# Second layer's projections: value products beside the rotated queries, biases added on 512 columns

## The chip, the cores and the metric

The kernel runs on one core of a Trainium2 chip. The metric is device time in microseconds (us), from launch to end. Engines: PE (TensorE, matrix products; PEld is its loading of weights), DVE (VectorE), ACT (ScalarE), POOL (GpSimd) and SP (SyncE, which issues DMAs here).

## The reference, cut to what matters

Four layers run one after the other on `x` of 4 x 512 x 256. The change is in the first part of the second layer. For each of four batches of 512 normalised tokens `xn` (256 features) this part computes:

```python
kv_d = xn @ Wkv_d.T + bkv_d          # 64 latent features
q_d  = xn @ Wq_d.T  + bq_d           # 64 latent features
k1 = kv_d @ Wk_u.T + bk_u            # 128
q1 = q_d  @ Wq_u.T + bq_u            # 128
v  = kv_d @ Wv_u.T + bv_u            # 256
kr = rope(xn  @ Wrk.T + brk)         # 128
qr = rope(q_d @ Wrq.T + brq)         # 128
S  = softmax(xn @ router_w + router_b)   # gates of 16 experts
y0 = xn @ expert_w + expert_b            # one product for all experts, 256
```

After it come the attention of 16 heads on `k = (k1, kr)`, `q = (q1, qr)` and `v`, and the addition of `y0` weighted by the gates.

## The kernel before, in words

Everything is written out by hand: each engine has its own list of instructions, run in order, and engines wait for one another by semaphores. A layer is made of blocks; at a block's end all engines meet.

`project1` is the block in question. It goes through the batches b = 0 to 3. Tokens are transposed to `xnT` (features on rows, 512 columns); `latT` holds `kv_d` on rows 0 to 63 (`LO`) and `q_d` on rows 64 to 127 (`HI`), and `w.up` holds the weights that act on each on the same rows. A product with only 64 contracted rows uses half of the array's rows.

PE's list for one batch is:

- the latent product (L837), 16 columns of router logits for each of four token tiles (L839), and the two halves of the rotary keys (L844, L845), all of 128 contracted rows;
- from `latT`: `k1` (L849, rows LO) and `q1` (L850, rows HI), then the two halves of the rotary queries (L851, L852, both rows HI), into banks 2 to 5;
- for each of four token tiles t: the expert product, 256 columns into the left half of bank 2 + t (L857), and the values, 256 columns into its right half (L858, rows LO). The banks are those of `k1`, `q1` and the two halves of `qr`, so each t first waits until that bank was read. After t = 1 come the transposes of the gates (L866). In the last batch the first two units of attention scores (L829) follow t = 2 and t = 3;
- the transposes of the next batch's `xn` into banks 0 and 1 (L814).

All matrix products that go through the helper `product` carry its line, L803. Each f32 matmul is two MATMUL instructions in the profile.

ACT's list for one batch: copy of the first half of `xnT` (L713), `latT` (L715), the exponential of the gates (L717), `k1` and `q1` with biases (L720, L722), normalising the next batch's `xn` (L707, four instructions), rounding of keys and queries to bf16: `kq1`, `kqr` (L702), then after POOL's subtractions the second parts, `kq1`, the gates' copy (L734), `kqr` (L702). POOL's list: the output bias for `x` (L674), reciprocal roots (L668), two subtractions (L688) and two more (L692), 1024 columns each. SP then stores the parts.

DVE's list for one batch: copy of the second half of `xnT` (L763), statistics of the next batch, logits and their maximum (L768 to L771), rotation of the keys (L755, L758, L760), the gates (L780 to L782), rotation of the queries (the same three lines), and for each tile t the biases of `y0` and `values` (L789, L790), 256 columns each. Eight maxima over score units (L794, two banks each) close the list of the block.

`attend1` is the block after it.

Of the kernel before, what the change touches and what calls it, by code (L numbers as in the profile page):

```python
# [9 lines left out]
ALU = mybir.AluOpType  # L10
# [3 lines left out]
P = 128  # L14
B, S, C = 4, 512, 256
# [34 lines left out]
class Core:  # L50
# [8 lines left out]
    def sem(self, name):  # L59
        return self.ctx.enter_context(self.nc.semaphore(name))  # L60
# [527 lines left out]
def project1(k, y0, gateT, values, split, early):  # L588
# [4 lines left out]
    PAIRS = TT * LANES // 2  # L593
    B_LAT, B_K, B_KR, B_KRS, B_Q, B_QR, B_QRS = (w.columns[:, i:i + 1] for i in range(7))
    V_ROW, O_ROW, E_ROW = range(3)
    with ExitStack() as ctx:
        sb, sem = scoped(k, ctx, "l1a")
        stats = sb("stats", [P, TT, 6])
# [33 lines left out]
        q1_ready = sem("q1_ready")  # L632
        qrot_done = sem("qrot_done")
        y_read = sem("y_read")
        lmax_ready = sem("lmax_ready")
        gexp_ready = sem("gexp_ready")
        gate_ready = sem("gate_ready")
# [100 lines left out]
        @block.vector  # L738
        def _(dve):
            own = Own(dve, dve_own)  # L740
            dve.wait_ge(*k.groups["w1"])

            def statistics(b):
                norm_stats(k, dve, own, lambda t: k.x[:, b, t, :], stats, mv, rstd, var_ready)

            def shifts(b):
                dve.wait_ge(rstd_ready, b)
                nc.vector.scalar_tensor_tensor(shift[:, :], mv[:, :, 0], -1.0, rstd[:, :], ALU.mult, ALU.mult).then_inc(shift_ready, 1)

            for b in range(B):  # L750

                def rotate(side, made, done, cos_bank, sin_bank, bias, swapped_bias):

                    dve.wait_ge(made, b * 2 + 1)
                    nc.vector.scalar_tensor_tensor(kqr[:, side, :], ps[cos_bank][:, :], bias, w.rope[:, 0, :], ALU.add,  # L755
                                                   ALU.mult).then_inc(done, 1)
                    dve.wait_ge(made, b * 2 + 2)
                    own.link(nc.vector.scalar_tensor_tensor(turn[:, side, :], ps[sin_bank][:, :], swapped_bias,  # L758
                                                            w.rope[:, 1, :], ALU.add, ALU.mult))
                    nc.vector.tensor_tensor(kqr[:, side, :], kqr[:, side, :], turn[:, side, :], ALU.add).then_inc(done, 1)  # L760

                dve.wait_ge(xt_made, b * 2 + 2)
                nc.vector.tensor_copy(xnT[:, 1, :], ps[1][:, :]).then_inc(xt_dve, 1)  # L763
                if b + 1 < B:
                    statistics(b + 1)

                dve.wait_ge(logits_made, b + 1)
                own.link(nc.vector.tensor_tensor(logit[:, :, :], ps[1][:, 0:TT * EXPERTS].rearrange("p (t e) -> p t e", t=TT),  # L768
                                                 w.router_b[:, :].unsqueeze(1).broadcast_to([P, TT, EXPERTS]), ALU.add))
                own.link(nc.vector.tensor_reduce(lmax[:, :], logit[:, :, :], axis=AX.X, op=ALU.max))  # L770
                nc.vector.tensor_tensor(logit[:, :, :], logit[:, :, :],  # L771
                                        lmax[:, :].unsqueeze(2).broadcast_to([P, TT, EXPERTS]),
                                        ALU.subtract).then_inc(lmax_ready, 1)
                if b + 1 < B:
                    shifts(b + 1)
                dve.wait_ge(biased, b + 1)
                rotate(0, kr_made, krot_done, 7, 0, B_KR, B_KRS)

                dve.wait_ge(gexp_ready, b + 1)
                own.link(nc.vector.tensor_reduce(lsum[:, :], logit[:, :, :], axis=AX.X, op=ALU.add))  # L780
                own.link(nc.vector.reciprocal(lsum[:, :], lsum[:, :]))
                nc.vector.tensor_tensor(logit[:, :, :], logit[:, :, :],  # L782
                                        lsum[:, :].unsqueeze(2).broadcast_to([P, TT, EXPERTS]),
                                        ALU.mult).then_inc(gate_ready, 1)
                rotate(1, qr_made, qrot_done, 4, 5, B_QR, B_QRS)

                for t in range(TT):
                    dve.wait_ge(y_made, b * TT + (t + 1))
                    nc.vector.tensor_tensor(y0[:, b, t, :], ps[2 + t][:, 0:C], w.rows[:, E_ROW, :], ALU.add)  # L789
                    nc.vector.tensor_tensor(values[:, b, t, :], ps[2 + t][:, C:2 * C], w.rows[:, V_ROW, :],  # L790
                                            ALU.add).then_inc(y_read, 1)
            for i in range(PAIRS):
                dve.wait_ge(early.smax_made, i + 1)
                nc.vector.tensor_reduce(early.nmax[:, 0, 2 * i:2 * i + 2], k.pair(early.bank(i)), axis=AX.X, op=ALU.max,  # L794
                                        negate=True).then_inc(early.smax_read, 1)

        @block.tensor
        def _(pe):
            pe.wait_ge(*k.groups["w1"])

            def product(bank, weights, rhs):
                for c in range(CT):
                    last = nc.tensor.matmul(bank, weights(c), rhs(c), start=(c == 0), stop=(c == CT - 1))  # L803
                return last

            LO, HI = slice(0, L1_LAT), slice(L1_LAT, P)
            def turn_input(b):
                if b:
                    pe.wait_ge(xn_ready, b)
                    pe.wait_ge(krot_done, b * 2 - 1)  # L810
                    pe.wait_ge(lmax_ready, b)
                for c in range(CT):
                    for t in range(TT):
                        last = nc.tensor.transpose(ps[c][:, t * P:(t + 1) * P], xn[:, t, c * P:(c + 1) * P], k.ident[:, :])  # L814
                    last.then_inc(xt_made, 1)

            def first_scores(i):
                if i == 0:
                    pe.wait_ge(early.loaded[0], LOADS)
                    pe.wait_ge(krot_done, B * 2 - 1)  # L820
                    pe.wait_ge(lmax_ready, B)
                elif i == 1:
                    pe.wait_ge(gt_ready, B)
                    pe.wait_ge(lat_ready, B)
                else:
                    pe.wait_ge(early.smax_read, i - 1)
                for m in range(2):
                    t, j = divmod(2 * i + m, LANES)
                    last = nc.tensor.matmul(ps[early.bank(i) + m][:, :], early.KQ[0:ROWS, QUERY, 0, j, t * P:(t + 1) * P],  # L829
                                            early.KQ[0:ROWS, KEY, 0, j, :], start=True, stop=True)  # L830
                last.then_inc(early.smax_made, 1)

            turn_input(0)
            for b in range(B):
# [10 lines left out]
                product(ps[0][:, :], lambda c: w.rope_k[:, c, P:2 * P], lambda c: xnT[:, c, :]).then_inc(kr_made, 1)  # L845
                pe.wait_ge(lat_ready, b + 1)
                if b:
                    pe.wait_ge(y_read, b * TT)
                nc.tensor.matmul(ps[2][:, :], w.up[LO, 0:P], latT[LO, :], start=True, stop=True).then_inc(k1_made, 1)  # L849
                nc.tensor.matmul(ps[3][:, :], w.up[HI, 0:P], latT[HI, :], start=True, stop=True).then_inc(q1_made, 1)  # L850
                nc.tensor.matmul(ps[4][:, :], w.up[HI, P:2 * P], latT[HI, :], start=True, stop=True).then_inc(qr_made, 1)  # L851
                nc.tensor.matmul(ps[5][:, :], w.up[HI, 2 * P:3 * P], latT[HI, :], start=True, stop=True).then_inc(qr_made, 1)  # L852

                for t, (ready, value) in enumerate(((k1_ready, b + 1), (q1_ready, b + 1), (qrot_done, b * 2 + 1),
                                                    (qrot_done, b * 2 + 2))):
                    pe.wait_ge(ready, value)
                    product(ps[2 + t][:, 0:C], lambda c: xnT[:, c, t * P:(t + 1) * P], lambda c: w.expert[:, c, :])  # L857
                    nc.tensor.matmul(ps[2 + t][:, C:2 * C], latT[LO, t * P:(t + 1) * P], w.up[LO, P:3 * P],  # L858
                                     start=True, stop=True).then_inc(y_made, 1)
                    if b + 1 == B and t >= 2:  # L860
                        first_scores(t - 2)
                    if t == 1:
                        pe.wait_ge(gate_ready, b + 1)
                        pe.wait_ge(krot_done, b * 2 + 1)
                        for u in range(TT):
                            last = nc.tensor.transpose(ps[7][0:EXPERTS, u * P:(u + 1) * P], logit[:, u, :], k.ident[:, :])  # L866
                        last.then_inc(gt_made, 1)
                if b + 1 < B:
                    turn_input(b + 1)
            for i in range(2, PAIRS):  # L870
                first_scores(i)
            pe.wait_ge(y_read, B * TT)
            pe.wait_ge(early.smax_read, PAIRS)


# [1715 lines left out]
```

## Time and profile before

| | before |
|---|---|
| median of 3 runs | 1127.55 us (1126.84 to 1127.59) |
| the profiled execution's own time | 1129.45 us |
| its span, first to last instruction | 1127.7 us |
| PE busy | 958.3 us, 85% |
| DVE busy | 793.3 us, 70% |
| POOL busy | 474.9 us, 42% |
| ACT busy | 462.9 us, 41% |
| mean granted PE clock | 0.936 |

The span is what the profile shows in detail; the 1.75 us between it and the execution's own time lie around it. Busy shares are averages over four layers with different limits, so what a change in one stage is worth has to be read from that stage. The granted clock is 1.00 at 2.4 GHz and 0.50 at 1.2 GHz.

### The profile page before, as it was taken

How to read it: one execution, taken by the hardware profiler on the slowest of the kernel's cores; microseconds unless marked ns; L12 is line 12 of the kernel's file. 1: busy time of each engine (PE TensorE's matmuls, PEld its weight loads, DVE VectorE, ACT ScalarE, POOL GpSimd, SP SyncE). 2: the span in 40 equal slices, each digit the busy share in tenths (PEclk: the TensorE clock that was granted, in tenths of full speed). 3: DMA queues.
4: the chain of work that ended last, by engine and by line, in shares of the span. 5: the costliest groups of instructions: out<-in, count | busy, mean ns of one | idle time of the engine just before them, and what ended most of it. 6: DMA issues, size and time to landing. Idle time of an engine off the chain costs nothing. (4 is left out here: it accounts for less than half of the span.)

```text
span 1127.7 us, 12859 instructions
## 1 busy us (share of the span) xinstructions
PE 958.3 (85%) x4126; PEld 497.0 (44%) x4130; DVE 793.3 (70%) x1395; ACT 462.9 (41%) x764; POOL 474.9 (42%) x479
## 2 busy tenths in 40 slices
PE   5899699799999998579999958887888788879877
PEld 2566455323333332336556544235533553355424
DVE  3665665688787875276877647993799378947795
ACT  3233145256666666264654426112621252124411
POOL 2322167464444440143633511961196108810781
PEclk9999899889999999599999969998999899999899
DMA  8500024312212200300000010000000000000000
GB/s 296 192 15 15 15 92 143 107 34 59 74 48 69 53 15 1 133 1 15 1 15 15 1 40 0 1 1 20 0 0 0 20 0 0 0 20 0 0 0 19
DMA packets 28653, 43.11 MB, mean 38 GB/s; under 512 B 6480, under 2 KB 21792, under 8 KB 28192
## 3 DMA queue, kind: packets, MB, share of 16 engines
q1 hardware_dynamic: 28592, 42.41, 12.0%
q8 instruction: 25, 0.41, 0.2%
q14 instruction: 36, 0.29, 0.1%
HBM read 30.93 MB, written 11.27 MB: 37 GB/s over the span
## 5 line engine op out<-in xcount | busy, mean ns | idle before, releaser
L1095 DVE TENSOR_REDUCE l_nmax<-banks 128x1 f32<-128x512 f32 (+1 forms) x165 | 147.9, 930 | 35.1 <-PE banks L1198 33.9
L1054 ACT ACTIVATE l1b_PT<-banks 128x512 f32<-128x512 f32 (+1 forms) x176 | 134.3, 794 | 66.7 <-PE banks L1211 66.2
L2431 PE MATMUL banks<-l_scaled,l_cbm 128*128 128x512 f32 x224 | 123.7, 667 | 41.5 <-POOL l_scaled L2141 23.7
L2141 POOL TENSOR_TENSOR l_scaled<-l_X,l_source 128x512 f32<-128x512 f32 x112 | 134.6, 1227 | 0.0
L2310 DVE TENSOR_TENSOR banks<-banks,l_decay 128x512 f32<-128x512 f32 x128 | 88.1, 691 | 12.2 <-PE banks L2431 7.7
L2431 PEld LDWEIGHTS banks<-l_scaled,l_cbm 128*128 128x128 f32 x224 | 40.0, 204 | 113.2 <-POOL l_scaled L2141 82.2
L1198 PE MATMUL banks<-l_KQ 96*128 96x512 bf16 x240 | 81.8, 394 | 8.0 <-DVE l_nmax L1095 5.2
L2284 DVE TENSOR_TENSOR l_y<-l_y,banks 128x512 f32<-128x512 f32 x128 | 86.7, 677 | 1.9
L1211 PE MATMUL banks<-l_KQ 99*128 99x512 bf16 x256 | 85.5, 388 | 2.9 <-ACT l1b_PT L1054 2.1
L2210 ACT ACTIVATE l_hhi<-l_h 128x512 f16<-128x512 f32 (+1 forms) x24 | 15.2, 632 | 137.7 <-DVE l_h L2323 137.7
L1225 PE MATMUL banks<-l1b_PT,l1b_V 128*32 128x512 f32 x512 | 68.2, 605 | 0.0
L2128 POOL TENSOR_TENSOR l_across<-l_X,l_source 128x512 f32<-128x512 f32 x16 | 17.0, 1075 | 120.9 <-ACT l_X L2196 120.9
L2240 DVE SCALAR_TENSOR_TENSOR l_conv<-l_padded,w_taps,l_conv 128x512 f32<-128x512 f32 x72 | 52.7, 750 | 15.2 <-ACT l_conv L2186 13.5
L1770 PE MATMUL banks<-l_xhi,l_ternary 128*128 128x512 f16 x128 | 49.5, 387 | 6.3 <-DVE l_h L1700 6.3
L1211 PEld LDWEIGHTS banks<-l_KQ 99*128 99x128 bf16 x256 | 22.3, 100 | 64.5 <-ACT l1b_PT L1054 47.8
L1563 POOL TENSOR_TENSOR l_sqsum<-l_sqsum,l_sq 128x512 f32<-128x512 f32 x28 | 40.3, 1440 | 23.3 <-ACT l_sq L1603 22.2
L1770 PE MATMUL banks<-l_xlo,l_ternary 128*128 128x512 f16 x128 | 49.4, 386 | 0.0
L2374 PE MATMUL banks<-l_xnT,w_inner 128*128 128x512 f32 x96 | 48.8, 671 | 0.0
L1757 PE MATMUL banks<-l_xnT,w_qkv 128*128 128x512 f32 x96 | 44.5, 622 | 1.0 <-DVE l_xnT L1644 1.0
L390 PE MATMUL banks<-w_qkv,l_xnT 128*128 128x512 f32 x64 | 37.0, 733 | 8.9 <-DVE l_xnT L289 8.9
L1021 POOL TENSOR_SCALAR l1b_above<-l1b_gate,l1b_trial 128x256 f32<-128x256 f32 x45 | 41.0, 924 | 1.4 <-DMA l1b_gate<-l_gate 1.4
L1198 PEld LDWEIGHTS banks<-l_KQ 96*128 96x128 bf16 x240 | 22.7, 99 | 40.1 <-DVE l_nmax L1095 14.9
(325 smaller groups left out, 2056.1 us busy)
## 6 DMA issues: line engine op xcount, KB each, us to landing
l_split<-l1a_parts SPq DMA_DIRECT2D x16, 384.0 KB, 3.3
l_KQ<-l_split SPq DMA_DIRECT2D x48, 128.0 KB, 2.9
l_KQ<-l_split SPq DMA_DIRECT2D x16, 192.0 KB, 3.1
l_KQ<-l_split SPq DMA_DIRECT2D x48, 64.0 KB, 2.8
w_ternary<-l_tern_out SPq DMA_DIRECT2D x7, 384.0 KB, 2.3
x<-in_x SPq DMA_DIRECT2D x4, 512.0 KB, 9.4
l_raw<-in_w_gate_up SPq DMA_DIRECT2D x2, 1024.0 KB, 10.3
out<-x SPq DMA_DIRECT2D x4, 512.0 KB, 3.0
```

Source lines behind the costliest of these rows:

```text
L1054: nc.scalar.activation(PT[:, first:first + size, :], source, ACT.Exp, scale=SCALE).then_inc(p_ready, 1)
L1095: nc.vector.tensor_reduce(nmax[:, H % 2, first:first + size], source, axis=AX.X, op=ALU.max, negate=True).then_inc(smax_read, 1)
L1198: last = nc.tensor.matmul(ps[bank + m][:, :], KQ[pairs, QUERY, g, j, t * P:(t + 1) * P], KQ[pairs, KEY, g, j, :], start=True, stop=True)
L1211: last = nc.tensor.matmul(ps[KEY_BANK + bank + m][:, :], KQ[whole, KEY, g, j, kt * P:(kt + 1) * P], KQ[whole, QUERY, g, j, :], start=True, ...
L1225: last = nc.tensor.matmul(ps[OUT_BANK][j * LANE:(j + 1) * LANE, :], V[:, kt, g * LANES + j, :], PT[:, kt * LANES + j, :], start=(kt == 0), ...
L1770: last = nc.tensor.matmul(ps[2 * (j % 2) + part][:, :], gate_up[:, c, first:first + P], x[:, c, :], start=(c == 0 and x is xhi), stop=(c = ...
L2141: nc.gpsimd.tensor_tensor(by_head(scaled[:, n % 4, :]), by_head(X[:, T, :]), spread(source[:, level, T, :]), ALU.mult).then_inc(scaled_rea ...
L2240: last = nc.vector.scalar_tensor_tensor(conv[:, n, :], padded[:, n % 2, tap:tap + S], w.taps[:, n, tap:tap + 1], conv[:, n, :], ALU.mult, ...
L2284: nc.vector.tensor_tensor(y[:, T, :], y[:, T, :], ps[4 + n % 4][:, :], ALU.add).then_inc(prod_added, 1)
L2310: nc.vector.tensor_tensor(by_head(ps[4 + n % 4][:, :]), by_head(ps[4 + n % 4][:, :]), spread(decay[:, level, T, :]), ALU.mult).then_inc(pr ...
L2374: last = nc.tensor.matmul(ps[2 + n][:, :], w.inner[:, c, X0 + n * P:X0 + (n + 1) * P], xnT[:, c, :], start=(c == 0), stop=(c == CT - 1))
L2431: last = nc.tensor.matmul(bank, cbm[:, T % 2, level, :], scaled[:, own_n % 4, :], start=True, stop=True)
```

## The change

In `project1` alone:

- The four value products of a batch leave the loop over t. Two of them (256 columns each, rows LO) are issued behind each of the two products of the rotary queries (512 columns, rows HI). They write both halves of bank 6, then of bank 1.
- The expert products of t = 0 and 1 share bank 2, those of t = 2 and 3 share bank 3. They wait for the reading of `k1` and `q1`.
- DVE adds the biases on 512 columns: two instructions for the values, then two for `y0`, where there were eight of 256 columns.
- New waits of PE: before the rotary queries, for the query rotation of the batch before and for the logits' last step (`lmax_ready`); before the transposes, for the values' addition (`v_read`); before the first score units, the same. The counts of `y_read` go from 4 to 2 a batch.

```diff
-                for t in range(TT):
-                    dve.wait_ge(y_made, b * TT + (t + 1))
-                    nc.vector.tensor_tensor(y0[:, b, t, :], ps[2 + t][:, 0:C], w.rows[:, E_ROW, :], ALU.add)
-                    nc.vector.tensor_tensor(values[:, b, t, :], ps[2 + t][:, C:2 * C], w.rows[:, V_ROW, :],
-                                            ALU.add).then_inc(y_read, 1)
+                for half in range(2):
+                    dve.wait_ge(v_made, b * 2 + (half + 1))
+                    nc.vector.tensor_tensor(values[:, b, 2 * half:2 * half + 2, :], halves(ps[V_BANKS[half]][:, :]),
+                                            w.rows[:, V_ROW, :].unsqueeze(1).broadcast_to([P, 2, C]), ALU.add).then_inc(v_read, 1)
+                for half in range(2):
+                    dve.wait_ge(y_made, b * 2 + (half + 1))
+                    nc.vector.tensor_tensor(y0[:, b, 2 * half:2 * half + 2, :], halves(ps[2 + half][:, :]),
+                                            w.rows[:, E_ROW, :].unsqueeze(1).broadcast_to([P, 2, C]), ALU.add).then_inc(y_read, 1)
...
+                    pe.wait_ge(v_read, b * 2)
...
+                    pe.wait_ge(v_read, B * 2)
                 elif i == 1:
                     pe.wait_ge(gt_ready, B)
                     pe.wait_ge(lat_ready, B)
+                    pe.wait_ge(v_read, B * 2 - 1)
...
                 if b:
-                    pe.wait_ge(y_read, b * TT)
+                    pe.wait_ge(y_read, b * 2)
                 nc.tensor.matmul(ps[2][:, :], w.up[LO, 0:P], latT[LO, :], start=True, stop=True).then_inc(k1_made, 1)
                 nc.tensor.matmul(ps[3][:, :], w.up[HI, 0:P], latT[HI, :], start=True, stop=True).then_inc(q1_made, 1)
-                nc.tensor.matmul(ps[4][:, :], w.up[HI, P:2 * P], latT[HI, :], start=True, stop=True).then_inc(qr_made, 1)
-                nc.tensor.matmul(ps[5][:, :], w.up[HI, 2 * P:3 * P], latT[HI, :], start=True, stop=True).then_inc(qr_made, 1)
-
-                for t, (ready, value) in enumerate(((k1_ready, b + 1), (q1_ready, b + 1), (qrot_done, b * 2 + 1),
-                                                    (qrot_done, b * 2 + 2))):
+                if b:
+                    pe.wait_ge(qrot_done, b * 2)
+                pe.wait_ge(lmax_ready, b + 1)
+                for turned in range(2):
+                    nc.tensor.matmul(ps[4 + turned][:, :], w.up[HI, (1 + turned) * P:(2 + turned) * P], latT[HI, :],
+                                     start=True, stop=True).then_inc(qr_made, 1)
+                    for t in (2 * turned, 2 * turned + 1):
+                        last = nc.tensor.matmul(ps[V_BANKS[turned]][:, t % 2 * C:(t % 2 + 1) * C], latT[LO, t * P:(t + 1) * P],
+                                                w.up[LO, P:3 * P], start=True, stop=True)
+                    last.then_inc(v_made, 1)
+
+                for t, (ready, value) in enumerate(((k1_ready, b + 1), (k1_ready, b + 1), (q1_ready, b + 1), (q1_ready, b + 1))):
                     pe.wait_ge(ready, value)
-                    product(ps[2 + t][:, 0:C], lambda c: xnT[:, c, t * P:(t + 1) * P], lambda c: w.expert[:, c, :])
-                    nc.tensor.matmul(ps[2 + t][:, C:2 * C], latT[LO, t * P:(t + 1) * P], w.up[LO, P:3 * P],
-                                     start=True, stop=True).then_inc(y_made, 1)
+                    last = product(ps[2 + t // 2][:, t % 2 * C:(t % 2 + 1) * C], lambda c: xnT[:, c, t * P:(t + 1) * P],
+                                   lambda c: w.expert[:, c, :])
+                    if t % 2:
+                        last.then_inc(y_made, 1)
```

## Rows read from the trace of the kernel before

**Rows 1.** Busy time by stretch: the block; columns PE, PEld, DVE, ACT, POOL, clock, DMA.
```profile
136.60:224.10 87.50, 78.09 (x304) 41.29 (x304) 53.80 (x122) 35.00 (x52) 54.95 (x36) 0.97 0.35 109
```

**Rows 2.** Timeline of PE, second batch: start us, us, then bracketed idle time.
```profile
157.64 1.96 PE L803 MATMUL banks<-l1a_xnT,w_latent 128*128 128x512 f32 x4 [0.87 <-DVE l1a_xnT L763]
159.44 1.85 PE L803 MATMUL banks<-w_router,l1a_xnT 128*128 128x16 f32 x16
161.14 3.68 PE L803 MATMUL banks<-l1a_xnT,w_rope_k 128*128 128x512 f32 x8
164.75 0.69 PE L849 MATMUL banks<-l1a_latT,w_up 64*128 64x512 f32 x1
164.76 0.69 PE L850 MATMUL banks<-l1a_latT,w_up 64*128 64x512 f32 x1
165.28 0.59 PE L849 MATMUL banks<-l1a_latT,w_up 64*128 64x512 f32 x1
...
165.72 1.02 PE L851 MATMUL banks<-l1a_latT,w_up 64*128 64x512 f32 x2
...
167.53 1.13 PE L803 MATMUL banks<-w_expert,l1a_xnT 128*128 128x256 f32 x4
168.59 0.70 PE L858 MATMUL banks<-w_up,l1a_latT 64*128 64x256 f32 x2
...
170.90 0.60 PE L866 MATMUL banks<-ident,l1a_logit 128*16 128x128 f32 x4
171.34 1.03 PE L803 MATMUL banks<-w_expert,l1a_xnT 128*128 128x256 f32 x4
...
174.61 1.09 PE L814 MATMUL banks<-ident,x 128*128 128x128 f32 x8
176.58 0.67 PE L803 MATMUL banks<-l1a_xnT,w_latent 128*128 128x512 f32 x1 [0.88 <-DVE l1a_xnT L763]
```

**Rows 3.** Timeline of ACT and POOL, from the second batch's `k1` to the next copy.
```profile
165.97 0.69 ACT L720 ACTIVATE l1a_kq<-banks,w_columns 128x512 f32<-128x512 f32 x1 [3.10 <-PE banks L849]
...
169.10 1.05 ACT L702 ACTIVATE l1a_parts<-l1a_kq 128x1024 bf16<-128x1024 f32 x1
...
170.23 2.13 POOL L688 TENSOR_TENSOR l1a_kq<-l1a_kq,l1a_parts 128x1024 f32<-128x1024 f32 x1 [6.75 <-ACT l1a_parts L702]
...
174.48 1.06 ACT L702 ACTIVATE l1a_parts<-l1a_kqr 128x1024 bf16<-128x1024 f32 x1 [0.55 <-POOL l1a_kqr L688]
...
175.44 0.58 ACT L713 ACTIVATE l1a_xnT<-banks 128x512 f32<-128x512 f32 x1
```

**Rows 4.** Timeline of DVE, second batch.
```profile
168.42 0.69 DVE L760 TENSOR_TENSOR l1a_kqr<-l1a_kqr,l1a_turn 128x512 f32<-128x512 f32 x1
...
175.74 0.69 DVE L763 COPY l1a_xnT<-banks 128x512 f32<-128x512 f32 x1 [0.27 <-PE banks L814]
```

**Rows 5.** Timeline of the block's end, last batch.
```profile
205.40 1.13 PE L803 MATMUL banks<-w_expert,l1a_xnT 128*128 128x256 f32 x4
...
209.97 0.57 ACT L734 ACTIVATE l_gateT<-banks 16x512 f32<-16x512 f32 x1
...
213.61 9.32 DVE L794 TENSOR_REDUCE l_nmax<-banks 128x2 f32<-128x1024 f32 x8
```

**Rows 6.** Waits of SP in the block: total, times, longest.
```profile
SPq L596 <- PEq L596: 4.1, 1, 4.1
```

**Rows 7.** Busy time by stretch around idle PE; columns as in rows 1.
```profile
37.10:39.86 2.76, 0.00 (x1) 0.03 (x1) 2.69 (x7) 0.00 (x0) 1.07 (x1) 1.00 0.96 261
40.62:44.04 3.42, 3.42 (x5) 1.35 (x4) 3.30 (x10) 0.66 (x2) 0.00 (x0) 0.50 0.39 158
503.31:505.45 2.14, 0.00 (x0) 0.00 (x0) 2.04 (x6) 0.81 (x2) 1.68 (x2) 1.00 0.00 0
777.90:788.14 10.24, 6.98 (x21) 4.95 (x22) 3.44 (x5) 1.47 (x2) 2.12 (x1) 0.50 0.01 2
781.16:784.80 3.64, 3.64 (x17) 3.64 (x18) 0.00 (x0) 1.00 (x1) 2.12 (x1) 0.50 0.00 0
1096.82:1099.27 2.45, 0.00 (x2) 0.01 (x1) 2.45 (x5) 1.25 (x3) 0.58 (x1) 1.00 0.00 0
```

More of the change, by code:

```diff
@@ L595, in project1 @@
     V_ROW, O_ROW, E_ROW = range(3)
+    V_BANKS = (6, 1)
     with ExitStack() as ctx:
@@ L634, in project1 @@
         y_read = sem("y_read")
+        v_made = sem("v_made")
+        v_read = sem("v_read")
         lmax_ready = sem("lmax_ready")
@@ L871, in _ @@
                 first_scores(i)
-            pe.wait_ge(y_read, B * TT)
+            pe.wait_ge(y_read, B * 2)
             pe.wait_ge(early.smax_read, PAIRS)
```

## The prediction

> **What bounds the kernel now.** I read the shares first and put them aside: they are averages over four layers. The table by stretch gives the block of the change 87.5 us, with PE busy 78.09 of them at a mean clock of 0.97 [rows 1]; the other layers are not touched and follow in sequence, so their times only shift. Then I read PE's timeline for one batch. From one latent product to the next are 176.58 - 157.64 = 18.94 us, and PE idles only once in them, 0.88 us, between the transposes and the next latent product, where DVE's copy L763 is the last of what it waits for [rows 2]. So PE paces the block. The question is what comes second, and how close behind.
>
> The timeline of ACT and POOL answers it [rows 3]. ACT waits for `k1` until 165.97. From there it has no slack: both additions and the normalising, then rounding at 169.10, which releases POOL at 170.23; POOL needs two subtractions of 2.13 us; ACT rounds the second part from 174.48, for which it waited 0.55 us on POOL; and only then, at 175.44, comes its copy of the next `xnT` in its list, done at 175.44 + 0.58 = 176.02. DVE's copy ends at 175.74 + 0.69 = 176.43 [rows 4]. The second path is 0.41 us behind the first. It starts at `k1` and does not contain one product that the change moves.
>
> **The change on PE.** A tile's step is now expert 168.59 - 167.53 = 1.06 us, then values up to the next expert. From the first expert to the transposes are 174.61 - 167.53 = 7.08 us, in which the gates' transposes take 171.34 - 170.90 = 0.44 [rows 2]. Each tile therefore takes (7.08 - 0.44)/4 = 1.66 us, of which the values hold 0.60. What an expert product costs without a change between whole and half array behind it, the rows show only through the latent product, four instructions of 512 columns in 159.44 - 157.64 = 1.80 us, so about 0.88 for 256 columns [rows 2]. After the change: 4 x 0.88 + 0.44 = about 4.0 us for 7.1, 3.1 us less on PE in a batch, if the values cost nothing in their new place.
>
> Do they? `k1` and `q1` are such a pair: rows LO and HI, first instructions at 164.75 and 164.76, both products done in 165.72 - 164.75 = 0.97 us, where the two rotary query products, both on rows HI, take 167.53 - 165.72 = 1.81 us [rows 2]. Two value products of 256 columns are as long as one rotary query product of 512. Lower bound nothing, as in the pair; upper bound their own time alone, 4 x 0.44 = 1.8 us a batch. I take nothing, the pair being the same kind of work on the same tile shapes.
>
> The Trainium skill speaks against that on its page "TensorE: Matmul & The Clock Gate" (section "The mechanism"): matmuls start and end strictly in program order. The trace disagrees for the two instructions of one product: the second of L849 starts at 165.28, behind the first of L850 at 164.76 [rows 2]. By the page's rule a value pair could begin only with the second half of its query product, which would cost some 0.6 us more a batch; this changes little below.
>
> The new waits of PE cost nothing. The query rotation of the batch before and `lmax_ready` are done long before. `v_read` stands before the transposes: DVE ends the query rotation at 168.42 + 0.69 = 169.11, then two additions of 0.69 us (the price of L760, 512 columns; upper bound 0.75, lower 0.58, L713's on ACT) give 170.5 [rows 3, 4]; the transposes would come at 167.53 + 4.0 = 171.5. The `y0` additions end near 172.3, within the 1.0 us of the transposes, so that DVE's copy isn't late. DVE's time goes from eight additions of 256 columns to four of 512, and is off the path either way.
>
> **What the loop gives.** The transposes end at 172.5 in place of 175.6, and DVE's copy at 173.2. ACT's copy remains at 176.02, because its whole chain hangs on `k1`. The next latent product starts some 0.12 us after that, at 176.14 in place of 176.58: the gain is about 0.4 us a batch, in three passages 1.2 us, not 3 x 3.1. (Lower bound 0, if ACT and POOL run a little slower beside a busier DVE; upper 3.1 each, if the chain weren't there.) The other 2.7 us become idle time of PE: 0.88 + 3.1 - 0.44 = 3.6 us at each passage.
>
> **The last batch** has no passage behind it. Counted in the time of before: experts from 205.40, two tiles to 207.2, gates' transposes to 207.6, the third tile to 208.5, score unit 0 (0.45 us) to 209.0, the fourth to 209.9. DVE's second `y0` addition goes from 210.0 to 210.7, and the first maximum starts there instead of at 213.61; score unit 1 waits for ACT's copy of the gates, which ends at 209.97 + 0.57 = 210.54, and is done at 211.1, in time for the second maximum [rows 5]. The eight maxima, 9.32 us, follow without a gap, so the block's end gains 213.61 - 210.7 = 2.9 us. SP's last store does not take it back: SP waited 4.1 us at the block's end [rows 6].
>
> Without anything else the sum is -1.2 - 2.9 = -4.1 us.
>
> **What idle time does to PE's clock.** Here I choose against the sum. Before the block, PE idled 2.76 us at 37.10 at a clock of 1.00; from 40.62, after it had resumed, the granted clock was 0.50 for 3.42 us with PE busy all the while [rows 7]. That is 1.2 in place of 2.4 GHz. Outside stretches where the clock was low already, the trace has fifteen idle stretches of PE of 2.39 us or more behind its first product, from that at 37.10 to that at 1096.82; all but the last were followed by such a drop, that one (2.45 us) kept 1.00 [rows 7]. Idle stretches near 2 us mostly keep it, as that at 503.31 does (2.14 us). The block has had none between batches. The change makes three, of 3.6 us each.
>
> The drop would cost half of what it covers of PE's work before `k1`, which is on the path: latent 1.8, router 1.7, rotary keys 3.6, `k1` 1.0, together 8.1 us [rows 2]. How long it lasts depends on what PE does. With dense products of 512 columns behind the gap it was 3.42 us, a cost of 1.7. With small products (16 instructions of 64 columns from 781.16 to 784.80) the low clock went on through them and 3.34 us into the dense products, to 788.14, 7.0 us after PE had resumed [rows 7]. Here 1.8 us of dense latent products come first, 3.6 at half clock, then the router's 16 instructions of 16 columns, 3.4 at half clock, then dense ones. If the clock returns during the latent products, a passage costs 1.7 us; if it stays for the router and 3.34 us more, 3.6 + 3.4 + 3.34 = 10.3 us low, it costs 5.1. I take the middle, 3.4, for some of each: 3 x 3.4 = +10.2 us. What PE does after `k1` may run slower too: it has 3.6 us to spare there.
>
> Forecast: -4.1 + 10.2 = +6.1 us. The profiled execution took 1129.45 us (span 1127.7 and 1.75 around it), so its like would be 1135.5; on the median 1127.55, which is 1.9 lower, 1133.6 us. With 1.7 at each passage it is +1.0 (1128.6), with 5.1 it is +11.2 (1138.8).
>
> **The rivals.** *The clock holds.* Then -4.1 us, 1123.5. For it: the idle stretch at 1096.82, and that the block's products are dense on both sides. Against: the fourteen others, and that 3.6 us is longer than half of them. Chance 0.10. *One drop in three, or all of them brief and late.* -4.1 + one passage of 1.7 to 5.1: within 2 us of now, 1125 to 1128.6. Chance 0.12. *The values are not hidden* but take 1.8 us a batch behind the queries. PE then idles 3.6 - 1.8 = 1.8 us at a passage, like the stretch that kept its clock; the loop still gains 1.2, the last batch 2.9 - 1.8 = 1.1: -2.3 us, 1125.3. Against it is the pair `k1`, `q1`. Chance 0.05. *ACT's chain is shorter than I read* (its order lets the copy through): each batch gains up to 3.1 us, -9.3 - 2.9 = -12.2, 1115.4. Against it: ACT's list is fixed in order, and the copy began at the very end of the rounding. Chance 0.03. The rest, 0.70, is the forecast: the sign turns where a passage costs more than 4.1/3 = 1.4 us, that is, where PE works 2.8 us at half clock before `k1` in each.
>
> **How the numbers follow.** What a measurement of this kernel can tell from no change is about 0.2%, 2.25 us. Of the forecast's 0.70, 0.61 lies above +2.25 and 0.09 within. Faster: 0.10 + 0.03 + half of 0.05, 0.15. Same: 0.12 + 0.09 + the other half, 0.23. Slower: 0.62. The likeliest case's own range is 1128.6 to 1138.8. The range of all reaches down to the case of hidden gains without a drop in part (1125.0) and up to the upper end with 2 us for a low stretch that falls worse into the start of the attention: 1141.0.
>
> **What would show it.** In the changed kernel's timeline: L849 and L851 at the same distance from the latent product wherever the clock is 1.00; value products beside L851's successors with the experts no later than 1.9 us after these begin; PE idle 3 to 3.7 us before each of three latent products, released by ACT's L713 and no longer by DVE's L763; 10.1 to 10.2 us from ACT's L720 to the end of L713, as now; and a granted clock of 0.50 over the latent products of batches 1 to 3. I am wrong if the clock stays at 1.00 there, if the idle time is under 2.4 us, or if L713 comes before ACT's last rounding.

## The result: faster, with the forecast on the wrong side

| | before | changed |
|---|---|---|
| median of 8 runs each, same chip | 1128.34 us (1126.84 to 1133.87) | 1123.37 us (1121.03 to 1127.02) |
| ratio | | 0.9956 (0.9936 to 0.9976) |
| the profiled execution's own time, span | 1129.45, 1127.7 us | 1127.02, 1125.2 us |
| mean granted PE clock | 0.936 | 0.932 |

The forecast was 1133.6 us, 6.1 slower; measured are 5.0 us less. The time is outside the range, 1125.0 to 1141.0 us, which left out two of the prediction's own rivals (1123.5 and 1115.4 us).

The first profile of the changed kernel happens to be the slowest of its eight executions. Its timeline of PE, second batch into the third (start us, us, idle time before in brackets; L809 is the helper that was L803):

```profile
156.76 3.23 PE L809 MATMUL banks<-l1a_xnT,w_latent 128*128 128x512 f32 x4 [3.58 <-ACT l1a_xnT L716]
...
161.96 3.68 PE L809 MATMUL banks<-l1a_xnT,w_rope_k 128*128 128x512 f32 x8
165.57 0.69 PE L858 MATMUL banks<-l1a_latT,w_up 64*128 64x512 f32 x1
...
166.53 0.38 PE L867 MATMUL banks<-w_up,l1a_latT 64*128 64x256 f32 x1
166.54 0.59 PE L864 MATMUL banks<-l1a_latT,w_up 64*128 64x512 f32 x1
...
168.35 1.99 PE L809 MATMUL banks<-w_expert,l1a_xnT 128*128 128x256 f32 x8
...
172.34 1.04 PE L821 MATMUL banks<-ident,x 128*128 128x128 f32 x8
176.88 2.87 PE L809 MATMUL banks<-l1a_xnT,w_latent 128*128 128x512 f32 x4 [3.50 <-ACT l1a_xnT L716]
```

Against [rows 2]: value products (L867) and rotary queries (L864) start together, though the values are listed behind both instructions of the query product, and queries and values take 168.35 - 166.53 = 1.82 us, as the queries alone did. PE now idles 3.5 us ahead of the latent product, and what ends the idle time is ACT's copy. ACT's timeline has the chain unchanged, 176.25 + 0.58 - 166.79 = 10.04 us against 10.05 in [rows 3]:

```profile
166.79 0.69 ACT L723 ACTIVATE l1a_kq<-banks,w_columns 128x512 f32<-128x512 f32 x1 [3.62 <-PE banks L858]
...
175.29 1.06 ACT L705 ACTIVATE l1a_parts<-l1a_kqr 128x1024 bf16<-128x1024 f32 x1 [0.55 <-POOL l1a_kqr L691]
176.25 0.58 ACT L716 ACTIVATE l1a_xnT<-banks 128x512 f32<-128x512 f32 x1
```

DVE's copy, last in [rows 4], is now done early. In the last batch the maxima start 218.82 - 210.80 = 8.02 us after `k1`, where it was 10.99 [rows 5, with `k1` at 202.62], and SP still waits for PE at the block's end, 1.2 us against 4.1 in [rows 6]:

```profile
173.42 0.69 DVE L766 COPY l1a_xnT<-banks 128x512 f32<-128x512 f32 x1 [0.18 <-PE banks L821]
...
218.82 9.32 DVE L800 TENSOR_REDUCE l_nmax<-banks 128x2 f32<-128x1024 f32 x8
```
```profile
SPq L597 <- PEq L597: 1.2, 1, 1.2
```

By stretches (span, busy time of PE, PEld, DVE, ACT, POOL, then clock and DMA) the block and its idle and low-clock stretches, to be read beside [rows 1, 7]:

```profile
133.41:229.81 96.40, 79.19 (x305) 48.26 (x305) 52.60 (x108) 34.92 (x52) 55.22 (x38) 0.82 0.35 99
153.20:156.76 3.56, 0.00 (x1) 0.00 (x1) 3.41 (x10) 2.95 (x4) 3.56 (x2) 1.00 0.00 0
157.36:160.78 3.42, 3.42 (x10) 1.86 (x8) 0.00 (x0) 0.69 (x1) 3.42 (x4) 0.50 0.80 262
177.84:188.08 10.24, 10.24 (x26) 6.10 (x24) 1.49 (x5) 0.94 (x2) 5.28 (x6) 0.50 0.55 172
201.72:208.56 6.84, 6.84 (x22) 4.76 (x21) 0.67 (x3) 0.94 (x2) 3.89 (x5) 0.50 0.68 230
```

So the mechanism forecast for the block is there: 3.5 us idle, and the clock at 1.2 GHz behind each. The block is not shorter but 8.6 us longer here. The gain must lie elsewhere. Cutting each profile at the first transposes of every part (the block ends at the next block's first product, which waits for POOL's `l1b_ident`) shows where. "Latent to `k1`" is the distance of the latent product from `k1` in the four batches; the lines below the first two are the experiments that follow:

| profile | block | latent to `k1` | third layer | fourth layer |
|---|---|---|---|---|
| before, first | 87.8 | 7.1, 7.1, 7.1, 7.1 | 194.5 | 463.9 |
| changed, first | 96.4 | 9.1, 8.8, 12.2, 10.5 | 191.6 | 460.3 |
| before, again | 87.9 | 7.1, 7.1, 7.1, 7.1 | 196.8 | 470.5 |
| changed, again | 88.4 | 7.1, 8.6, 8.8, 8.8 | 191.7 | 460.5 |
| changed, third | 88.4 | 7.1, 8.7, 8.8, 8.8 | 191.8 | 460.6 |
| changed, 16 memsets, first | 96.3 | 9.1, 8.8, 12.2, 10.5 | 192.8 | 465.2 |
| changed, 16 memsets, again | 88.3 | 7.1, 8.6, 8.8, 8.8 | 193.0 | 465.6 |
| before, wide additions | 88.9 | 7.1, 7.1, 7.1, 7.1 | 191.4 | 460.3 |

The fourth layer, whose code is the same, is 3.6 to 10 us shorter. It is the only part written as a loop over the batches. DVE's first copy in it, over the run before, four times (idle time ahead of it in us, and how often):

```profile
L2234 DVE COPY l_xnT<-banks x4: 691/692/692, 665.9 to 1012.2; 128x512 f32<-128x512 f32 x4
its engine sat idle before it (us, times) until:
  issue: 14.8, 3
```

In the changed kernel's third profile the same copy (the "issue" sums are of the copies into this tile alone):

```profile
L2251 DVE COPY l_xnT<-banks x4: 692/692/693, 660.6 to 1004.9; 128x512 f32<-128x512 f32 x4
its engine sat idle before it (us, times) until:
  issue: 8.4, 3
```

At each of the three turns of the loop DVE stood 4.9 us before and stands 2.8 us now, and it waited for nothing that the profile shows ("issue"). PE waits for that copy.

### The profile page after: what moved, and what is told of

Read it like the earlier page. It is cut to its first block and busy times, and to the rows that moved or that the text cites. A ratio compares the mean times of both kernels' runs of the same rounds, so it can differ in the third digit from the quotient of the medians.

```text
span 1125.2 us, 12850 instructions
## 1 busy us (share of the span) xinstructions
PE 951.4 (85%) x4126; PEld 499.1 (44%) x4130; DVE 793.8 (71%) x1379; ACT 461.5 (41%) x764; POOL 474.4 (42%) x479
## 5 line engine op out<-in xcount | busy, mean ns | idle before, releaser
L390 PE MATMUL banks<-w_qkv,l_xnT 128*128 128x512 f32 x64 | 32.0, 648 | 8.8 <-DVE l_xnT L289 8.8
```

## The experiments

### What in the change makes it faster

**Sixteen memsets back (e1_pad, and e10_pad beside e9_after).** DVE's list is 16 instructions shorter in the changed kernel. This puts 16 back, four per batch (0.08 us each four):

```diff
                                         ALU.subtract).then_inc(lmax_ready, 1)
+                for i in range(4):
+                    nc.vector.memset(spare[:, i:i + 1], 0.0)
```

> The changed kernel with sixteen more instructions in DVE's list of the block (four memsets of one spare column per batch, behind the logits' last step, where DVE has about 1 us to spare), so that DVE's list in front of the fourth layer's loop is as long as before the change (967 instructions, against 951 in the changed kernel). Theory A (the change was faster because the loop of the fourth layer now stands elsewhere in DVE's list: its first copy waits 2.6 to 2.8 us at each of three turns, put down to issue, where before it waited 4.8 to 5.1): the long waits come back, 3 x 2.2 = 6.7 us, so about 1130 us, slower than the kernel before by about 2. Theory B (the time was won in the block itself, the fourth layer's waits are chance): nothing changes, 1123.4 us, 5 less than before.

Measured: 1128.98 us, ratio to before 0.9982 (0.9960 to 1.0003). The gain is gone; that it would be 2 us slower than before did not show. Since the changed kernel had been timed on another chip, both were timed again on one:

> The changed kernel, unchanged, timed beside the next one on the same chip: 0.994 to 0.996 of the kernel before, 1123 us. Its block in a third profile: 88 to 97 us, with the latent product's start preceded by 3.5 us of idle PE and a clock of 0.50 over it in two or three of three passages.

> The changed kernel with the sixteen memsets again, so that DVE's list of the fourth layer stands where it stood before the change; on the same chip as the changed kernel itself. Theory A (the gain lies in the fourth layer's turns): 4 to 7 us slower than the changed kernel, and within 0.3% of the kernel before, since the block costs between +0.5 us (passages at 8.7 us, as in the changed kernel's second profile) and +8.6 us (as in its first). Theory B: no slower than the changed kernel.

Measured: changed 1121.83 us, 0.9938 (0.9911 to 0.9965); with the memsets 1129.08 us, 0.9990 (0.9967 to 1.0014). Sixteen memsets cost 7.3 us, and the waits at the turns are back:

```profile
L2254 DVE COPY l_xnT<-banks x4: 692/692/692, 663.6 to 1011.8; 128x512 f32<-128x512 f32 x4
its engine sat idle before it (us, times) until:
  issue: 14.9, 3
```

The change itself, with the list where it was, makes no difference that can be measured.

**The wide additions alone (e2_wide).** PE's list as before; DVE adds over pairs of banks:

```diff
-                for t in range(TT):
-                    dve.wait_ge(y_made, b * TT + (t + 1))
...
+                for half in range(2):
+                    dve.wait_ge(y_made, b * TT + 2 * half + 2)
+                    made = k.pair(2 + 2 * half)
+                    nc.vector.tensor_tensor(y0[:, b, 2 * half:2 * half + 2, :], made[:, :, 0:C],
+                                            w.rows[:, E_ROW, :].unsqueeze(1).broadcast_to([P, 2, C]), ALU.add)
```

> The kernel before with only the second part of the change: biases added on 512 columns (left halves of banks 2 and 3 as one instruction, right halves as one, then banks 4 and 5), PE's list as before. DVE's list is 16 instructions shorter. Theory A: the fourth layer's turns lose 3 x 2.2 = 6.7 us, the block loses up to 0.3 us at each passage because the last two additions (0.69 us each) end behind the transposes; together about 6, 1122.5 us, with PE's own part of the change absent. Theory B (the gain is in PE's reordered products): 1128 to 1129 us, as before.

Measured: 1122.38 us, 0.9926 (0.9899 to 0.9954). The reordered products are not needed for the gain. The block is 1.1 us longer than before (88.9 against 87.8), a little more than expected: 0.5 us by three periods of 19.11 us against 18.94, the rest at its ends.

### What the idle time costs, and what bounds the block

**The idle time filled (e3_fill).** Behind the transposes of each next batch:

```diff
+                if b:
+                    for _ in range(3):
+                        nc.tensor.matmul(ps[5][:, :], w.up[:, 0:P], w.rope[:, 0, :], start=True, stop=True)
```

> The changed kernel with three idle-time products (f32, 512 columns, constant operands, into bank 5, whose result nobody reads) behind the transposes of batches 1 to 3: 2.6 us of PE work in the 3.5 us in which PE would idle. Theory C (the idle time lowers PE's clock and this costs 3.4 us a passage, 1.7 to 5.0 in the profile of the changed kernel): the clock stays at 1.00 over the latent products, the distance from latent product to k1 is 7.1 us again, and the time falls by 5 to 10 us, to about 1115. If the drop costs little in most executions, the time stays at 1123.

Measured: 1114.54 us, 0.9858 (0.9828 to 0.9887), 9 us less than the changed kernel by the medians, which were taken on two chips; the changed kernel's one execution on this chip took 1122.46 us, 8 us more. PE's timeline of this kernel, second passage:

```profile
168.98 1.04 PE L821 MATMUL banks<-ident,x 128*128 128x128 f32 x8
169.85 2.74 PE L825 MATMUL banks<-w_rope,w_up 128*128 128x512 f32 x6
173.53 0.70 PE L809 MATMUL banks<-l1a_xnT,w_latent 128*128 128x512 f32 x1 [0.94 <-ACT l1a_xnT L716]
```

and its block in the table by stretches:

```profile
134.53:218.00 83.47, 73.24 (x323) 43.94 (x324) 53.13 (x108) 34.93 (x52) 55.32 (x38) 0.97 0.39 114
```

The clock holds between the batches, periods are 18.46 to 18.52 us, latent to `k1` 7.1 in all four. The block is 4.4 us shorter than before; the sum without the clock was -4.1. Useless products make the kernel faster. Against the changed kernel's second and third profile the block is 4.9 us shorter, against its first 12.9 us; the rest of the 9 us lies outside the block and its cause isn't shown.

**ACT's copy ahead (e4_order), and the shifts behind the rotation (e5_shift).**

```diff
+                if b + 1 < B:
+                    copy_turned(b + 1)
                 act.wait_ge(rest_ready, b * 2 + 1)
                 round_part(b, 0, kq1, 1, second_ready)
```

> The changed kernel with ACT's copy of the next xnT moved ahead of its two last roundings, into the time in which ACT waits for POOL. Theory D (the path behind PE is ACT's list from k1 over POOL's two subtractions to that copy, 10.1 us): DVE's copy is again last, PE idles under 2.4 us, the clock holds, and the batch takes 16 to 17 us instead of 18.5 plus the clock's cost; then POOL and DVE's rotations bound it. 3 x (2 + 3.4) = 16 us less, about 1107. Rival: POOL's list alone needs the time, the passage stays near 18.5 and the time within 3 us of 1123.

Measured: 1114.73 us, 0.9848 (0.9812 to 0.9885), less of a gain than expected. The profiled execution (1117.86 us) is one of the slower of the six, 1109.63 to 1118.70. Its second passage shows why, in the timeline of DVE, and below it in that of PE:

```profile
164.11 0.16 DVE L756 SCALAR_TENSOR_TENSOR l1a_shift<-l1a_mv,l1a_rstd 128x4 f32<-128x4 f32 x1 [3.65 <-POOL l1a_rstd L671]
```
```profile
171.73 1.60 PE L826 MATMUL banks<-ident,x 128*128 128x128 f32 x8 [2.41 <-DVE l_values L797]
```

With a shorter period DVE waits for POOL's reciprocal root ahead of the rotation, the values are added late, and `v_read`, the wait that the change added, holds the transposes. PE idles 2.41 us, the clock falls, and that batch has 12.8 us from latent to `k1`. So:

```diff
-                if b + 1 < B:
-                    shifts(b + 1)
                 dve.wait_ge(biased, b + 1)
                 rotate(0, kr_made, krot_done, 7, 0, B_KR, B_KRS)
+                if b + 1 < B:
+                    shifts(b + 1)
```

> As the kernel with ACT's copy moved ahead (1114.7 us), and DVE computes the next batch's shifts behind the rotation of the keys instead of ahead of it. In that kernel's profile the second passage still had PE idle 2.41 us, because DVE waited 3.6 us for POOL's reciprocal root ahead of the rotation and so added the values late; the clock fell for 13.7 us and the passage took 21.5 us. Theory: without that wait in front of the rotation the transposes are not late, PE idles under 1 us at each passage (released by DVE's copy), the clock stays at 1.00 behind the first batch, and the three passages take 16 to 16.5 us each, against 18.93 before the change: block 87.8 - 3 x 2.7 - 2.9 = about 77, time about 1107 us. Rival: another list (POOL's four operations and the bias, 12.3 us a batch, or ACT's second roundings) bounds it near 17.8 to 18.5 us a passage, and the time is 1110 to 1113.

Measured: 1107.01 us, 0.9812 (0.9786 to 0.9838). The passages take 15.79 us each, the block 75.5; PE is the bound again:

```profile
164.67 1.04 PE L826 MATMUL banks<-ident,x 128*128 128x128 f32 x8
166.58 1.96 PE L814 MATMUL banks<-l1a_xnT,w_latent 128*128 128x512 f32 x4 [0.88 <-DVE l1a_xnT L771]
```
```profile
133.00:208.50 75.50, 66.30 (x305) 40.91 (x306) 55.13 (x108) 34.58 (x52) 55.30 (x38) 0.95 0.41 126
```

This is what the change is worth once the second path is moved out of its way: 18.94 - 15.79 = 3.15 us a passage, and I had estimated 3.1 us less on PE. The kernel before with these two moves alone was not run; PE idled only 0.88 us a batch in it.

**Both kernels once more, for second profiles (e7_before, e8_after).**

> The kernel before once more, unchanged, for a second profile. Where the clock falls in the first, third and fourth layer differs from execution to execution; the block has no drop before its last scores (87.8 us again within 0.3), and the waits at the fourth layer's turns are 4.8 to 5.1 us again. If the change's gain in the fourth layer were chance, these waits would differ here.

> The changed kernel once more, unchanged, for a second profile. The first one was the slowest of its eight executions. If the cost of the clock in the block differs between executions, the distances from latent product to k1 differ from 8.8, 12.2 and 10.5 us here and the block is shorter than 96.4 us (92 if a passage costs 1.7 to 3); if it is always the same, they repeat.

Measured in single runs: 1134.61 and 1122.46 us. The waits at the turns are 5.1, 4.9 and 4.9 us before, 2.6 to 2.8 in the changed kernel. The clock's cost in the block does differ: here it falls for 3.4 us a passage, 1.5, 1.7 and 1.7 us of latent to `k1`, and the block is 88.4 us. The timeline and the stretch of the third passage:

```profile
176.56 3.65 PE L809 MATMUL banks<-l1a_xnT,w_latent 128*128 128x512 f32 x4 [3.50 <-ACT l1a_xnT L716]
```
```profile
176.74:180.14 3.40, 3.40 (x6) 1.33 (x6) 0.30 (x1) 0.00 (x0) 3.40 (x4) 0.50 1.02 286
```

### Why sixteen instructions count

By the written lists, DVE's first copy of the fourth layer is its instruction 967 before and 951 in the changed kernel, counted from 0; the loop has some 283. The DMA queues at the first turn of the kernel before (packets, MB, share of 16 engines), from 1.5 us ahead of the transposes to 5 us behind their start:

```profile
q1 hardware_dynamic: 528, 0.52, 23.9%
q14 instruction: 2, 0.02, 0.7%
```

The store of `x` goes out at just this turn (528 packets on its queue), with instruction packets on both sides of it. These start at 775.89 and 778.61 us, the store's packets start between 776.37 and 778.0, and DVE starts at 780.32. In the changed kernel's third profile the first two instruction packets start at 776.22 and 777.56, both ahead of the store's first at 777.75, and DVE starts at 779.50. The second packets, each in a window of half a microsecond, 778.23 to 778.73 before and 777.12 to 777.62 in the changed kernel:

```profile
q14 instruction: 1, 0.01, 3.8%
```
```profile
q14 instruction: 1, 0.01, 3.9%
```

In all their profiles, at every turn, DVE's copy starts 1.7 to 2.1 us behind the second packet. So 4.9 us against 2.8 goes with whether the store stands between the two packets; no run without the store tests it. More memsets move the loop on:

> The kernel before with sixteen more instructions in DVE's list (the same memsets): the fourth layer's first copy of DVE stands at 983 instead of 967. If what counts is the position within a stretch of 32 instructions, it is as good as the changed kernel's 951: the waits at the three turns are 2.6 to 2.9 us and the time about 6 less than before. If a longer list is simply a later one, or a longer stretch counts, the waits stay at 4.8 to 5.1 us and the time at 1128 to 1130.

> The kernel before with 64 more instructions in DVE's list; the fourth layer's first copy stands at 1031. Known are 951 (waits of 2.6 to 2.9 us), 967 (4.8 to 5.1) and 983 (1.6). If the position within a stretch of 64 counts, the waits are those of 967 again, 4.8 to 5.1 us. If it is within 32, the same; if only a longer stretch counts, they are others.

> The kernel with ACT's copy ahead and the shifts behind the rotation (1107.0 us), with 32 memsets of a spare column added to DVE's list, so that the fourth layer's first copy stands at 983, where the padded kernel before had it (waits at the turns of 1.6 us, put down to PE, in place of 2.6 to 2.9; fourth layer 455.4 us in place of 460). Theory: 4 to 5 us less, 1102 to 1103 us, 0.977 of the kernel before. If the position acted only together with the old PE list: 1107 again.

At 983 the kernel before takes 1121.04 us, 0.9933 (0.9901 to 0.9964), and DVE waits 1.64, 1.63 and 1.63 us, for PE's transposes:

```profile
775.68 0.69 DVE L2237 COPY l_xnT<-banks 128x512 f32<-128x512 f32 x1 [1.64 <-PE banks L2366]
```

No instruction packets run at its turns. At 1031 it is the same, 1.63 us (1121.27 us in one run), so the period is neither 32 nor 64, with which 1031 would be as slow as 967. On top of the best kernel, position 983 brought nothing: 1108.56 us, 0.9810 (0.9781 to 0.9838), though its waits fell to 1.6. Its fourth layer took 463.1 us in the profile against 460.4, with PE's clock low for about 76 us in it against 56, summed over the stretches. That expectation was a miss: a shorter turn also moves where the clock falls.

What was left: a longer period, 128 or 256, the length alone, or something short. With memsets at the head of DVE's list, in the first layer:

> The kernel before with 256 memsets of spare columns at the head of DVE's list in the first layer, where DVE waits for its data; the fourth layer's first copy stands at 1223 = 967 + 256. Theory F (DVE's list is fetched in blocks of 256, two of them stay, and the loop of 283 instructions is refetched at each turn when it touches three; the Trainium skill's page "Runtime: NRT & Kernel Launch", section "Instruction fetch mechanics", says so): the long waits come back, 4.8 to 5.1 us at three turns, with instruction packets on the DMA queue beside the store of x, and the time is 1128 to 1134 us. Rival (the waits belong to the old length alone): 1.6 us as at 983 and 1031, time 1118 to 1122.

> The same with 160 memsets; the fourth layer's first copy stands at 1127. Theory F: 967 and 951 touch three blocks, 983 to about 1200 touch two, so here the waits at the turns are 1.6 us, no instruction packets run there, and the time is 1118 to 1122 us. Rival (a period of less than 256 that 951, 967, 983 and 1031 happen to fit): some longer wait, 2.6 to 5.1 us.

Measured at 1223: 1133.78 us, 1.0044 (1.0030 to 1.0058), waits of 5.15, 5.07 and 4.96 us, instruction packets back at each turn. The medians are 4.8 us apart. The block starts at 139.74 us here and at 132.98 to 138.37 in the other profiles, so a part of them is what 256 memsets cost in the first layer. The queues at its first turn:

```profile
q1 hardware_dynamic: 528, 0.52, 24.0%
q14 instruction: 2, 0.02, 1.1%
```

At 1127: 1122.13 us, 0.9909 (0.9875 to 0.9943), waits of 1.68, 1.63 and 1.62 us, and the queues of its first turn are

```profile
q1 hardware_dynamic: 528, 0.52, 23.8%
```

951, 967 and 1223 are slow, 983, 1031 and 1127 fast. That fits a fetch in blocks of 256 of which DVE keeps two: a loop of 283 touches either two or three. The Trainium skill, on its page "Runtime: NRT & Kernel Launch" (section "Instruction fetch mechanics"), gives these two figures and says that a taken branch to a target outside the two blocks has to wait for a fetch; the six positions agree on one condition. A loop of 283 touches three blocks of 256 only when a block begins among its first 26 instructions, so one would have to begin between about 968 and 977. My count from 0 puts the starts of blocks at 768 and 1024; some 50 instructions that I didn't count would have to stand ahead of DVE's list.

The packets say more. The program's share of this queue, first in the kernel before, then in that at 983:

```profile
q14 instruction: 36, 0.29, 0.1%
```
```profile
q14 instruction: 21, 0.17, 0.1%
```

All other kernels at 951 and 967 have 36 packets too, the one at 1223 has 38, the others at 983, 1031 and 1127 have 21 or 22. The difference of 15 is five in each of the three rounds behind a turn. Memsets in DVE's list alone make them come and go, so they are DVE's. Counted in DVE's recorded instructions from the loop's first copy (279 a round), three come at the turn, and the other two at 126 and 251 before the change, at 19 and 143 behind it, where the list stands 16 earlier. The one at 951 + 19 = 970 lies where the block has to begin.

The size of a block stays open. Each of these packets has 8 KB, and they come some 125 recorded instructions apart. Blocks of 128 of which three are kept would fit the six positions as well, since no position 128 behind 967 (1095) was run.

## Why the prediction was wrong

**Two steps failed.** The one that turned the sign is the first paragraph's "the other layers are not touched and follow in sequence, so their times only shift". They are not touched, but DVE's list ahead of them became 16 instructions shorter, and that moved the fourth layer's loop to a better place: 4.9 us of waiting at a turn became 2.8, three times, 6.5 us (14.9 - 8.4) of DVE's time, 7.3 us of the kernel's. The profile of before had the wait: a copy of DVE with 4.8 to 5.1 us of "issue" ahead of it at each turn, which I saw only as PE's idle stretches with a clock drop behind them.

**The block** by its own steps:

- The values beside the rotated queries cost nothing: right, 1.82 us for both. The first value product starts at 166.53, 0.01 us ahead of the query product that is listed before it, so strict program order, which the prediction priced at 0.6 us, doesn't hold here either.
- ACT's chain from `k1` is second and does not shorten: right, 10.04 us; idle time 3.5 to 3.6 us, as worked out; period 18.50 us where the clock held, against 18.94.
- The last batch gains 2.9 us: right, 10.99 - 8.02 = 2.97. The sum without the clock, -4.1 us: right, -4.4 in the kernel with filled idle time.
- The clock falls at each passage: right, in nine passages of nine of the changed kernel's three profiles.
- Its price, 3.4 us as a middle of 1.7 and 5.1: the second step that failed, a term mis-sized. Two of three profiles have 1.5 to 1.7 us, the lower bound, so the block is +0.6 us and not +6.1; the first has 1.7, 5.0 and 3.4 with a low first batch (2.0) beside them, +8.6. The same two pictures appear in the kernel with 16 memsets. Why an execution shows one or the other isn't shown; the dear one also has the clock low in the first batch, and the median is near the times of the cheaper one (1122.46 and 1120.98 us).

With the price at its lower bound (1.7 us, three times, in place of 3.4) the forecast would have been 6.1 - 5.1 = +1.0 us, and with 6.5 to 7.3 us less for the code's place -5.5 to -6.3: measured -5.0.

The measured 1123.4 us is also almost the number of the rival "the clock holds", 1123.5. That is chance: the clock fell at every passage, and the two errors made up for it.

**Left open.** The third layer takes 194.5 and 196.8 us before and 191.6 to 191.8 in the changed kernel. It is not the position alone (190.9 to 196.8 us in the kernels at 983 and beyond). In the second profile of before, DVE had 6.1 us of "issue" ahead of one instruction there, and 5.8 us in the kernel at 1127; both have the longest third layer, 196.8 us. And the fourth layer's first batch is 118.3 us in the changed kernel against 111.9 and 118.1 in the two profiles before, with the clock low for about 25 us of it against 12 and 25. So the fourth layer of single profiles doesn't give the 7 us (3.6 to 10); they come from the medians of kernels timed side by side.

## What to carry to other kernels

Before taking work off the engine that bounds a loop, find the path behind it, from the last common product to the engine's next start; if it is 0.4 us behind, the engine gains 0.4 us and idle time for the rest, and the idle time can cost PE its clock. Move the second path first: here that made the same change worth 21 us instead of 5 (both with some 7 us of the code's place in them). And look at every turn of a written loop for waits put down to issue: their length can hang on how many instructions stand ahead in that engine's list, so an edit anywhere earlier in it can give or take microseconds that have nothing to do with it. A few memsets tell the two apart.

## What the runs showed of the hardware

- A loop of some 283 DVE instructions waited 4.8 to 5.2 us at a turn at two positions 256 apart, 2.6 to 2.9 at a third, and not at all beyond PE at three others. At the slow positions five instruction packets of 8 KB came in each further round, at the others none; the long waits had the store of 512 KB between the first two of them, the shorter ones had it behind both.
- Dummy f32 products of 2.6 us in 3.5 us of idle time kept the granted clock at 1.00 (2.4 GHz) between the batches and went with 8 to 9 us less time, 4.9 or 12.9 of the block.
- Two value products on rows 0 to 63 and one query product of twice the length on rows 64 to 127 ran side by side, pass by pass: 1.82 us for both, where the queries alone took 1.81, though the list has the query product first.
